# Second-layer tiles regrouped around t's pairs, low and high parts reordered, and a second root path for the last tile

## The reference

```python
h = _ln(_ln(x, pw_g[pathway_ids], pw_b[pathway_ids]), cp_g[compartment_ids], cp_b[compartment_ids])
t = _ln(x, tm_g[time_steps], tm_b[time_steps])
m, n, r = [x + _mlp_ln(state_i, ...)[:, None, :] for each of three states]
s = _ln(x, ms_g[scale_type], ms_b[scale_type])
cat = concatenate([w[0]*h, w[1]*t, w[2]*m, w[3]*n, w[4]*r, w[5]*s], axis=-1)
out = x + _ln(silu(cat @ int_W1 + int_b1) @ int_W2 + int_b2, int_g, int_be)
```

## Time and profile before

| | |
|---|---|
| median of 3 runs (lowest to highest) | 951.33 us (950.12 to 954.25) |
| profiled execution, its own time | 952.21 us |
| its span, first to last instruction | 950.5 us |
| mean granted TensorE clock | 0.997 |
| busy: PE, PEld, DVE, ACT, POOL | 97%, 78%, 87%, 34%, 47% |

### The profile page before, as it was taken

How to read it: one execution, slowest core, us unless ns; L and a number is a source line. 1 busy time by engine, 2 the same in 40 slices (tenths; PEclk the granted TensorE clock), 3 DMA queues, 4 the chain that set the end, 5 groups by cost and what they waited for, 6 DMA issues and landing times.

```text
span 950.5 us, 13455 instructions
## 1 busy us (share of the span) xinstructions
PE 923.2 (97%) x4166; PEld 745.4 (78%) x4166; DVE 825.8 (87%) x1199; ACT 326.0 (34%) x415; POOL 449.8 (47%) x576
## 2 busy tenths in 40 slices
PE   7999999999999999999999999999999999999997
PEld 6767887878888787887878878787887878788785
DVE  6899898898889889898889988889888988989855
ACT  5835224242332514224242332424233251432411
POOL 6355463643636454363644435355363645436122
PEclk9999999999999999999999999999999999999999
DMA  9984667648475674757657475774847667485432
GB/s 327 353 296 142 207 170 254 168 127 247 125 235 162 192 217 114 241 131 254 177 148 231 141 241 133 244 175 124 253 122 243 156 190 219 113 249 125 125 88 65
DMA packets 99618, 178.75 MB, mean 188 GB/s; under 512 B 10128, under 2 KB 49040, under 8 KB 95632
## 3 DMA queue, kind: packets, MB, share of 16 engines
q1 hardware_dynamic: 44656, 96.07, 29.0%
q0 software_dynamic: 22976, 66.07, 28.8%
q10 hardware_dynamic: 31968, 16.39, 5.9%
HBM read 145.75 MB, written 32.75 MB: 188 GB/s over the span
## 4 chain that ended last, share of the span: by engine, by line
DVE 35%; issue 34%; PE 13%; POOL 11%; ACT 3%; DMA 2%; DVEq 1%; POOLq 1%; ACTq 0%; SPq 0%
DVE yst L1096 4%; DVE y_sb L1093 4%; DVE y_sb L1112 4%; DVE xc L1014 3%; DVE r_sb L1175 3%; DVE v_ring L1059 3%; PE hid_ps L1567 3%; PE hid_ps L1568 3%; PE hid_ps L1569 3%; POOL pw_rows L619 3%; DVE y_sb L1084 2%; POOL pw_rows L612 2%; POOL frs L541 2%; DVE fst L1128 2%; DVE cat_lo L1064 2%
## 5 line engine op out<-in xcount | busy, mean ns | idle before, releaser
L1567 PE MATMUL hid_ps<-cat_hi,w_hi 128*128 128x512 f32 x1008 | 397.1, 394 | 14.1 <-DVE cat_lo L1064 14.1
L1568 PE MATMUL hid_ps<-cat_lo,w_hi 128*128 128x512 f32 x1008 | 393.1, 390 | 0.0
L1569 PE MATMUL hid_ps<-cat_hi,w_lo 128*128 128x512 f32 x1008 | 392.9, 390 | 0.0
L1567 PEld LDWEIGHTS hid_ps<-cat_hi,w_hi 128*128 128x128 f32 x1008 | 189.5, 188 | 66.3 <-DVE cat_lo L1064 21.5
L1569 PEld LDWEIGHTS hid_ps<-cat_hi,w_lo 128*128 128x128 f32 x1008 | 189.6, 188 | 39.9
L1568 PEld LDWEIGHTS hid_ps<-cat_lo,w_hi 128*128 128x128 f32 x1008 | 189.7, 188 | 38.4
L612 POOL DMA_INDIRECT pw_rows<-pw,path_now x64 | 77.2, 1206 | 91.6 <-DVE y_sb L1112 75.4
L619 POOL DMA_INDIRECT pw_rows<-cp,class_now x64 | 93.4, 1459 | 36.8 <-issue 17.3
L633 POOL DMA_DIRECT2D r_sb<-x x60 | 57.3, 955 | 106.4 <-DVE r_sb L1175 103.3
L853 ACT ACTIVATE z_sb<-hid_ps,batch_bias 128x512 f32<-128x512 f32 x64 | 43.8, 691 | 168.9 <-PE hid_ps L1569 168.9
L835 ACT ACTIVATE cat_hi<-v_ring 128x1024 fp32r<-128x1024 f32 x30 | 31.9, 1062 | 154.1 <-DMA v_ring<-h_turned 154.1
(11 more groups left out here) (187 smaller groups left out, 1414.4 us busy)
## 6 DMA issues: line engine op xcount, KB each, us to landing
x_sb<-xp SPq DMA_DIRECT2D x16, 1024.0 KB, 5.2
out<-r_sb SPq DMA_DIRECT2D x63, 256.0 KB, 2.0
xc<-xT SPq DMA_DIRECT2D x15, 1024.0 KB, 6.9
h_turned<-y_sb ACTq DMA_DIRECT2D x60, 256.0 KB, 6.5
r_sb<-x POOLq DMA_DIRECT2D x60, 256.0 KB, 4.6
v_ring<-h_turned SPq DMA_DIRECT2D x60, 256.0 KB, 3.3
stats_bc<-token_stats SPq DMA_DIRECT2D x15, 512.0 KB, 5.6
ids_sb<-ids SPq DMA_DIRECT2D x16, 256.0 KB, 5.3
```

Source lines behind the costliest of these rows:

```text
L1567: pe.matmul(acc, w1_hi[:, k, cols], hi, start=start, stop=False)
L1568: pe.matmul(acc, w1_hi[:, k, cols], lo, start=False, stop=False)
L1569: return pe.matmul(acc, w1_lo[:, k, cols], hi, start=False, stop=stop)
```

## The change

On PE, in batches 2 to 15, `second(b - 1, 0)` and `second(b - 1, 1)` stand ahead of pair 2, and `second(b - 1, 2)` and `second(b - 1, 3)` behind pairs 2 and 3; none stands behind pairs 4 and 5. On DVE `hidden_low` 1 follows `hidden_low` 0, ahead of `ts_mult` 0, and `ts_low` 0 stands ahead of `y_turn` 1. On ACT `hidden_high` 1 stands ahead of all four `y_hat`, and both `hinges` ahead of `h_write`. In batch 1 only DVE changes, where `ts_low` 0 stands ahead of `y_norm` 2 and 3. For the last output tile, the root is taken by ACT (`Sqrt`, with one such call ahead to have its table) and DVE (`reciprocal` and a Newton step, four small instructions) in place of POOL's two.

```diff
--- before.py
+++ after.py
@@ -147,6 +147,7 @@
         fmv = sb("fmv", [P, TT, 2])
         fve = sb("fve", [P, TT])
         frs = sb("frs", [P, TT])
+        last_cols = sb("last_cols", [P, 5])
         net_g = sb("net_g", [NR, D])
         nst = sb("nst", [P, 6])
         nmv = sb("nmv", [P, 2])
@@ -297,6 +298,10 @@
 
         last_hi_done = sem("last_hi_done")
         last_stored = sem("last_stored")
+        root_tabled = sem("root_tabled")
+        last_root = sem("last_root")
+        last_var = sem("last_var")
+        last_step = sem("last_step")
         last_lo_done = sem("last_lo_done")
         x_offset = sem("x_offset")
         b2_cleared = sem("b2_cleared")
@@ -720,7 +725,7 @@
             pool.tensor_tensor(class_tab[32:33, :], b2_bc[32:33, :], class_tab[32:33, :].bitcast(f32),
                                ALU.subtract).then_inc(b2_ready, 1)
             pool.wait_ge(b2_ready, 1)
-            for t in range(TT):
+            for t in range(TT - 1):
                 out_rstd(BATCHES - 1, t)
 
         @block.scalar
@@ -936,16 +941,14 @@
                     h_write(b)
                     ts_high(b, 3)
                 else:
-                    y_hat(b, 0)
-                    y_hat(b, 1)
                     hidden_high(b - 1, 1)
-                    y_hat(b, 2)
-                    y_hat(b, 3)
+                    for t in range(TT):
+                        y_hat(b, t)
                     ts_high(b, 0)
                     ts_high(b, 1)
                     hinges(b, 2)
+                    hinges(b, 3)
                     h_write(b)
-                    hinges(b, 3)
                     ts_high(b, 2)
                     ts_high(b, 3)
                 if first:
@@ -973,6 +976,9 @@
             chunk(BATCHES - 1, last=True)
             for h in range(FT):
                 last_hidden(h)
+            act.activation(last_cols[:, 0:1], eps_col[:, 0:1], ACT.Sqrt).then_inc(root_tabled, 1)
+            act.wait_ge(faggr, TT * BATCHES)
+            act.activation(last_cols[:, 1:2], fmv[:, TT - 1, 1:2], ACT.Sqrt, bias=eps_col[:, 0:1]).then_inc(last_root, 1)
             act.wait_ge(out_ready, TT * BATCHES + 1)
             act.dma_start(out_v[BATCHES - 1][:, TT - 1, D // 2:D], r_sb[:, TT - 1, D // 2:D]).then_inc(last_stored, 16)
 
@@ -1153,8 +1159,25 @@
                 dve.wait_ge(faggr, n)
 
                 dve.wait_ge(out_ready, n - 2)
+                if t < TT - 1:
+                    dve.scalar_tensor_tensor(o_sb[:, t % 2, :], second_ps[t], fmv[:, t, 0:1], g_bc,
+                                             ALU.subtract, ALU.mult).then_inc(fnum, 1)
+                    return
+
+                dve.tensor_tensor(fve[:, t:t + 1], fmv[:, t, 1:2], eps_col[:, t:t + 1], ALU.add).then_inc(last_var, 1)
                 dve.scalar_tensor_tensor(o_sb[:, t % 2, :], second_ps[t], fmv[:, t, 0:1], g_bc,
                                          ALU.subtract, ALU.mult).then_inc(fnum, 1)
+
+                about, off, rest = [last_cols[:, i:i + 1] for i in range(2, 5)]
+                dve.wait_ge(last_root, 1)
+                dve.reciprocal(about, last_cols[:, 1:2]).then_inc(last_step, 1)
+                dve.wait_ge(last_step, 1)
+                dve.wait_ge(last_var, 1)
+                dve.scalar_tensor_tensor(off, about, about, fve[:, t:t + 1], ALU.mult, ALU.mult).then_inc(last_step, 1)
+                dve.wait_ge(last_step, 2)
+                dve.tensor_scalar(rest, off, -0.5, 1.5, ALU.mult, ALU.add).then_inc(last_step, 1)
+                dve.wait_ge(last_step, 3)
+                dve.tensor_tensor(frs[:, t:t + 1], rest, about, ALU.mult).then_inc(frs_done, 1)
 
             def last_sum(t):
                 n = TT * (BATCHES - 1) + t + 1
@@ -1348,9 +1371,9 @@
                     y_norm(b, 1)
                     ts_mult(b, 0)
                     ts_mult(b, 1)
+                    ts_low(b, 0)
                     y_norm(b, 2)
                     y_norm(b, 3)
-                    ts_low(b, 0)
                     ts_low(b, 1)
                     ts_mult(b, 2)
                     hidden_low(b - 1, 0)
@@ -1363,16 +1386,16 @@
                     for t in range(TT):
                         y_norm(b, t)
                     hidden_low(b - 1, 0)
+                    hidden_low(b - 1, 1)
                     ts_mult(b, 0)
                     y_turn(b, 0)
                     ts_mult(b, 1)
+                    ts_low(b, 0)
                     y_turn(b, 1)
-                    ts_low(b, 0)
                     y_turn(b, 2)
                     y_turn(b, 3)
                     ts_low(b, 1)
                     ts_mult(b, 2)
-                    hidden_low(b - 1, 1)
                     ts_mult(b, 3)
                     ts_low(b, 2)
                 if not last:
@@ -1711,13 +1734,17 @@
                 batch_turn()
                 last_pairs(0, 3)
 
-            def chunk(b, last=False):
+            def chunk(b, first=False, last=False):
                 first_pair(b)
                 fill_and_bias(b)
                 pair(b, 1)
+                if not first:
+                    second(b - 1, 0)
+                    second(b - 1, 1)
                 for n in range(TS0, H0):
                     pair(b, n)
-                    second(b - 1, n - TS0)
+                    if first or n < H0 - 2:
+                        second(b - 1, n - TS0 + (0 if first else 2))
                 for h in range(FT):
                     last_pairs(b, h)
                 if last:
@@ -1725,7 +1752,7 @@
                         last_second(t)
 
             first_chunk()
-            chunk(1)
+            chunk(1, first=True)
             with pe.Fori(0, BATCHES - 3) as i:
                 chunk(i + 2)
             chunk(BATCHES - 1, last=True)
```

## The result

The changed kernel takes 945.04 us (median of 5 runs, 943.76 to 945.90) against 952.51 us for the kernel before in the same comparison: a ratio of 0.9923, 95% interval 0.9903 to 0.9942. It is faster by 0.8%, where I had forecast +1.8 us, 953.1. The measured time lies inside the forecast's range of 941 to 963, but on the other side of the kernel before. Profiled, it ran 945.04 us with a span of 943.3 us, 7.2 us less than the span before. The granted TensorE clock was 0.999 against 0.997, and over the 13 passes it reads 1.00 in both profiles, so it is no part of the difference.

What follows compares the result with a forecast made beforehand. The prediction took DVE, in a loop with ACT and POOL, as the bound. It summed -2.3 (PE's lag) + 3.4 (loop period) + 0 + 0.7 (tail) = +1.8 us, from 951.33 to 953.1 us, range 941 to 963.

Steps and rivals of the forecast that it cites:

- What bounds the kernel before: DVE, in a loop with ACT and POOL, sets a 56.6 us batch period; PE needs about 55.5 us.
- The rival in which PE is the bound: PE's stalls at pair 2 go, -14.3 us, tail adds 0.7: 937.7 us; chance 0.06.
- PE let go 2.3 us earlier, once: PE's wait moves from pair 2 to `second`, ending 2.3 us earlier relative to DVE: -2.3 us once, bounds 0 and -2.3.
- The loop's period: `h_write` on ACT starts 2.0 us later, so DVE's `ts_low` 2 slips: +0.26 us a pass, +3.4 us over 13.
- the lag of PE: PE's lag behind DVE shrinks once, not per batch; PE arrives early and waits for DVE's next period: -2.3 us.
- I am wrong if DVE starts to wait for PE: Sign against the forecast in the new profile: DVE, taken as the bound, would begin waiting for PE.
- The tail: After the last numerator, dependent small DVE instructions delay the last sum: +0.7 us, bounds 0 and 1.2; POOL's instructions no longer waited for.
- Rival 1: `h_write`'s issues take 3.03 us instead of 4.04, shortening DVE's period: -11.4 us, 939.9; chance 0.17 including part-way.
- Rival 3: Turned rows land late, DVE waits before `y_mul` every pass: 963.5 us; chance 0.25 including a longer issue to the same effect.
- The first batch's edit: `ts_low` 0 ahead of two `y_norm` in batch 1 moves 1.1 us within DVE's queue once: 0, bounds -1 and +1.

Runs made afterwards that it cites:

- The filler: Kernel before plus one needless 0.69 us DVE instruction ahead of `h_low` 0 in the 13 loop passes: 966.48 us, ratio 1.0093; on the changed kernel 945.28 us.
- the first experiment: Kernel before with one edit, both `hinges` ahead of `h_write` on ACT, PE, DVE and tail untouched: 937.47 us, ratio 0.9836.
- the two kernels that open it: Changed kernel with second-layer tiles moved behind pair 4: both from behind pairs 2 and 3, 940.20 us (0.9857); only the last, from behind pair 3, 938.10 us (0.9855).

## Why the prediction was wrong

- *What bounds the kernel before: right.* The filler and the first experiment show it: 0.60 us a pass for an instruction of 0.63. The rival in which PE is the bound falls, though the change was faster. The tiles moved into PE's stall did not bring the gain: with them and without the hinges' edit the kernel is slower.
- *PE let go 2.3 us earlier, once: right.* The wait moved to `second`, 3.54 us behind `hidden_low` 0 (487.92 - 484.38), where 490.13 - 486.58 = 3.55 had been worked out. The stretch from batch 15 to the last matmul is 2.3 us shorter.
- *The loop's period: the step that failed.* "`h_write` starts at 491.82 + 0.97 + 1.42 + 1.42 = 495.63." It took ACT's queue for one line, as the opening does with "the same queues", in which an issue starts only once all that stands ahead has run. The kernel before had been no proof of that: there `h_write` waited for the last `y_turn` anyway. Measured, it starts with the end of the last `y_turn`, 8.18 us behind `hidden_low` 0 and not 9.05, so the hinges cost the chain nothing. In this pass `ts_low` 2 comes 1.2 us earlier than before, not 0.2 to 0.3 later. Of this, 1.1 are lost to the later `y_turn`, 1.9 gained since only `ts_high` 2 stands between the issues and DVE, and 0.5 are a shorter `h_write` (3.54 against 4.04). Of the 1.45 us by which I missed, the early start of the issues is 0.87 and their shorter length 0.50. The prediction had the length open between 3.03 and a longer stretch, and on which side it would fall was chance.
- *The gain given back: a second step that failed.* On average over the 13 passes `ts_low` 2 comes 13.04 us behind `hidden_low` 0, where it was 14.01: 0.97 us earlier, which is 12.6 us in all. The loop gained 4.0. I had treated the lag of PE as something that feeds nothing back to DVE. But four tiles now stand ahead of the end of pair 4, where there were two, and `x_high` of the next batch waits for that. This ring holds the pass at 56.13 us. It is the new bound, and the two kernels that open it are 0.5 and 0.7% below the changed kernel's median. The sign "I am wrong if DVE starts to wait for PE" came true in this way, through ACT: in DVE's 10 waits at `x_low`.
- *The tail: the term right, the end missed.* The last sum came 0.67 us later behind the statistics; 0.7 was forecast. "POOL's two small instructions of that tile are simply no longer waited for" missed that the end of the program waits for POOL, which gave 1.9 us back.
- *Rival 1* had the right sign by the wrong cause. `h_write` was a little shorter in some passes (3.1 to 4.3 us, 3.7 on average), but after the change its length no longer sets the pass. *Rival 3*: `y_mul` waited for the turned rows 0.9 us in all. It was near, and it did not decide; where their lateness shows is `h_low`, with 7.0 us in 10 waits of the loop.
- *The first batch's edit*, taken at 0 with bounds of 1 us, shows as no more than the +0.3 us up to batch 2. It was not tried alone. Nor were the moves of `hidden_high` 1 and `hidden_low` 1 apart from PE's order, nor the tail's edit on the changed kernel: its 1.2 us are read beside the hinges' edit and from the two profiles. What lengthens and shortens `h_write`, 3.1 to 4.3 us in the changed kernel, stays open too.

## What to carry to other kernels

When a change has several parts, cost each alone as well as together: here one moved line was worth 1.6%, and the rest of the change, built around PE's largest stall, cost 0.7% without it. A wait that goes from an engine which is not the bound is worth its lag once. After moving work on an engine with slack, follow each release that it gives, slots of a ring above all, until the path comes back: a period that was the same to 0.02 us in ten of 13 passes was the mark of such a closed path here.

## What the runs showed of the hardware

- A DMA issue on ScalarE's queue starts while an activation that stands ahead of it is still waiting to run: at 492.56 us against 492.70 for the last hinge in the changed kernel, and at 485.10 against 485.55 with the hinges' edit alone. What stands behind the issues does wait for them: `ts_high` 2 for 2.63 us. The "Advanced Engine Details and Errata" page of the Trainium skill (Engine Queue Depths) gives ScalarE a queue of 8 instructions. The rows agree with a queue between the two; its depth they don't show.
- The end of the program waits for POOL. Where POOL's last instruction stood beside the last sum, the span ended 5.1 us behind that instruction, which is 5.0 us behind the start of the sum (4.3 where the sum started 0.7 later). With POOL's last work 3.8 us ahead of the sum (936.4 against 940.2) it ended 3.1 us behind the sum's start.
- The root that DVE waits for in `out_sum` stands behind three gathers in POOL's queue. In every trace of this case DVE waited 1.8 us where the first of them took 3.1 us or more, and under 1 us where it took 2.6 or less.
